# K-nearest-neighbour blocks on one core: neighbour marks turned by DMA instead of TensorE, and the last batch's square row moved to step 0

## What is computed

```python
def _L0_xattn_ref(xyz, points, w_center, w_neighbor):
    ...
    idx = _knn_indices(xyz, K)                 # K = 8 smallest of sq_n + sq_m - 2 x_n.x_m
    idx_t = jnp.transpose(idx, (0, 2, 1))[:, None, :, :]
    for i in range(NUM_BLOCKS):                # 4 blocks
        shortcut = points
        p = _lrelu(points)
        g = _group_point(p, idx_t)             # the 8 neighbours of every point
        c = jnp.einsum('oi,bin->bon', w_center[i], p)
        gn = jnp.einsum('oi,bikn->bokn', w_neighbor[i], g)
        points = (c + gn.sum(axis=2)) / (K + 1.0) + shortcut
    return points
...
    x = _L0_xattn_ref(ctx_4096, x, fside_BxSxS_0, fside_BxSxS_0)
    x = _L1_xattn_ref(ctx_4096, x, fside_BxSxS_0, fside_BxSxS_0)
```

## Time and profile before

| | |
|---|---|
| time, median of 3 runs | 337.64 us (336.52 to 339.07) |
| profiled execution | 334.24 us, of which the span of its instructions is 332.5 us |
| TensorE busy | 320.8 us, 97% of the span |
| VectorE / ScalarE / GpSimd busy | 258.5 / 174.0 / 95.0 us |
| 64 transposes of marks (L385) on TensorE | 4.3 us busy |
| 8 copies `adj<-wide` (L538) on ScalarE | 7.7 us busy |
| DMA | 23.41 MB, nearly all of it in the first 90 us |

### The profile page before, as it was taken

How to read it: one execution, slowest core, us unless ns; L and a number is a source line. 1 busy time by engine, 2 the same in 40 slices (tenths; PEclk the granted TensorE clock), 3 DMA queues, 4 the chain that set the end, 5 groups by cost and what they waited for, 6 DMA issues and landing times.

```text
span 332.5 us, 5114 instructions
## 1 busy us (share of the span) xinstructions
PE 320.8 (97%) x2024; PEld 290.9 (88%) x2024; DVE 258.5 (78%) x333; ACT 174.0 (52%) x255; POOL 95.0 (29%) x85
## 2 busy tenths in 40 slices
PE   4999999999999899999899999999999999999995
PEld 4999999999899788888788889888888888889884
DVE  3994799799699676888867796887869867796773
ACT  4584397485564726454836644626455264644510
POOL 2011111111133214333644441426335063441400
PEclk9999999999999999999999999999999999999999
DMA  7979859969700000000000000000000000000023
GB/s 236 353 209 264 223 146 239 279 150 251 188 0 1 2 0 2 0 0 2 1 2 0 1 3 0 0 2 0 2 0 0 2 0 2 0 0 2 38 92 126
DMA packets 8608, 23.41 MB, mean 70 GB/s; under 512 B 772, under 2 KB 2052, under 8 KB 8584
## 3 DMA queue, kind: packets, MB, share of 16 engines
q1 hardware_dynamic: 7288, 18.36, 16.3%
q0 software_dynamic: 1296, 4.72, 8.3%
HBM read 20.98 MB, written 2.10 MB: 69 GB/s over the span
## 4 chain that ended last, share of the span: by engine, by line
PE 41%; DVE 8%; ACT 2%; issue 1%; DVEq 0%
PE wide L423 24%; PE wide L412 6%; PE wide L401 5%; PE wide L399 5%; DVE y_rest L722 2%; DVE y_lo L726 2%; DVE r_mixed L662 2%; DVE state L734 2%; ACT y_hi L570 2%; ACT relu L562 1%; PE wide L385 0%; ACT r_high L565 0%; DVEq L709 0%; DVEq L725 0%
## 5 line engine op out<-in xcount | busy, mean ns | idle before, releaser
L279 POOL TENSOR_TENSOR r_low<-relu,r_high 128x512 fp32r<-128x512 f32 x64 | 84.8, 1339 | 140.4 <-ACT r_high L565 140.4
L423 PE MATMUL wide<-adj,y_hi 128*128 128x512 f32 (+1 forms) x260 | 102.3, 394 | 0.8 <-DVE state L734 0.8
L423 PE MATMUL wide<-adj,y_lo 128*128 128x512 f32 (+1 forms) x260 | 101.7, 393 | 0.0
L722 DVE TENSOR_TENSOR y_rest<-wide,y_hi 128x1024 f32<-128x1024 f32 x32 | 39.2, 1224 | 45.4 <-ACT y_hi L570 45.4
L562 ACT ACTIVATE relu<-state 128x512 f32<-128x512 f32 x64 | 40.2, 628 | 46.5 <-DVE state L734 33.7
L399 PE MATMUL wide<-w_high,r_high 128*128 128x256 f32 x256 | 62.2, 281 | 0.9 <-DVE y_rest L722 0.9
L401 PE MATMUL wide<-w_low,r_low 128*128 128x256 f32 x256 | 61.9, 280 | 0.0
L570 ACT CAST y_hi<-wide 128x1024 fp32r<-128x1024 f32 x32 | 32.3, 1008 | 54.8 <-PE wide L401 54.8
L423 PEld LDWEIGHTS wide<-adj,y_hi 128*128 128x128 f32 x260 | 48.9, 188 | 11.7 <-DVE state L734 1.2
L423 PEld LDWEIGHTS wide<-adj,y_lo 128*128 128x128 f32 x260 | 49.0, 188 | 10.5 <-issue 0.2
L399 PEld LDWEIGHTS wide<-w_high,r_high 128*128 128x128 f32 x256 | 48.3, 189 | 2.3 <-issue 1.1
(11 more groups left out here) (57 smaller groups left out, 290.6 us busy)
## 6 DMA issues: line engine op xcount, KB each, us to landing
raw<-in_ctx_dram SPq DMA_DIRECT2D x23, 512.0 KB, 5.4
g_low<-in_ctx_dram POOLq DMA_DIRECT2D x9, 512.0 KB, 6.2
state<-in_x_dram SPq DMA_DIRECT2D x4, 512.0 KB, 7.1
out_dram<-state SPq DMA_DIRECT2D x3, 512.0 KB, 2.8
w_raw<-in_fside_BxSxS_dram SPq DMA_DIRECT2D x1, 1024.0 KB, 11.2
rest_raw<-in_ctx_dram SPq DMA_DIRECT2D x4, 130.0 KB
raw<-in_ctx_dram SPq DMA_DIRECT2D x2, 256.0 KB, 3.3
out_dram<-state SPq DMA_DIRECT2D x1, 256.0 KB, 2.0
```

What stands on the lines that cost most here:

```text
L279: nc.gpsimd.tensor_tensor(r_low[:, n % 3, h, :], relu[:, h, :], r_high[:, n % 3, h, :].bitcast(fp32), ALU.subtract).then_inc(r_low_ready, 1)
L423: mm = nc.tensor.matmul(bank[to][:, cols], part[:, s % 2, q, h * P:(h + 1) * P], adj[:, b, q, cols], start=(q == 0 and part is y_hi), stop ...
L722: nc.vector.tensor_tensor(y_rest[:, :, :], wide[MAIN][:, :].rearrange("p (q o) -> p q o", q=NB), y_hi[:, s % 2, :, :].bitcast(fp32), ALU.s ...
```

## The change

The marks are turned by `dma_start_transpose` from `nbr` to a new SBUF tensor `turned`: four DMAs of 128x512 bf16 (128 KB each) per batch, issued by SyncE. ScalarE copies `adj` from `turned`. TensorE's `turn_neighbours` is gone and with it the use of banks 6 and 7 by the marks, so `square_row(b)` waits on `low_copied` in place of `adj_ready`. In SyncE's queue the DMAs for batch 0 stand ahead of the loads of batch 3; those for batches 1, 2 and 3 stand behind all loads. Each set waits for `self_added(b)` and, from batch 1 on, for the copies of the batch before. `copy_adj` comes after `copy_low` in the Gram phase. In the layer phase the work of batch 3 moves one step forward (`square_row` and `distances` to step 0, `turn_distances` and `copy_low` to step 1, `neighbours` to steps 2 to 5, marks to 4 and 6, `add_selves` to 6, `copy_adj(3)` to 8), and `copy_adj(2)` moves one step back, to step 1 behind `copy_low(3)`.

```diff
+        turned = sb("turned", [P, NB, N], bf16)
...
+            def turn_neighbours(b):
+
+                sp.wait_ge(self_added, b + 1)
+                if b > 0:
+                    sp.wait_ge(adj_ready, 2 * b)
+                for i in range(NB):
+                    sp.dma_start_transpose(turned[:, :, i * P:(i + 1) * P], nbr_rows[:, i, :]).then_inc(nbr_turned, 16)
...
             for b in range(1, B):
+                if b == B - 1:
+                    turn_neighbours(0)
                 for k in range(UNITS):
                     load_unit(b, k)
                 load_state(b - 1)
             load_state(B - 1)
+            for b in range(1, B):
+                turn_neighbours(b)
...
             def square_row(b):
 
                 if b > 0:
-                    pe.wait_ge(adj_ready, 2 * b)
+                    pe.wait_ge(low_copied, b * NB)
...
             for b in range(B):
                 main_products(b, 0)
-                if b >= 2:
-                    turn_neighbours(b - 2)
...
                 if s == 0:
-                    turn_neighbours(B - 2)
+                    square_row(B - 1)
                 if s == 1:
-                    square_row(B - 1)
                     pe.wait_ge(gram_ready, B * NB)
...
-                if s == 2:
+                if s == 1:
                     turn_distances(B - 1)
-                if s == ENTER - 1:
-                    turn_neighbours(B - 1)
...
             def copy_adj(b):
+                act.wait_ge(nbr_turned, 16 * NB * (b + 1))
                 for g in range(2):
-                    act.wait_ge(nbr_turned, 2 * b + g + 1)
-                    nc.scalar.copy(adj[:, b, 2 * g:2 * g + 2, :],
-                                   bank[TR_BANKS[g]][:, :].bitcast(bf16).rearrange("p (j n) -> p j n", j=2))\
-                        .then_inc(adj_ready, 1)
+                    nc.scalar.copy(adj[:, b, 2 * g:2 * g + 2, :], turned[:, 2 * g:2 * g + 2, :]).then_inc(adj_ready, 1)
...
                 points_parts(b, 6)
+                copy_low(b - 1)
                 if b >= 2:
                     copy_adj(b - 2)
-                copy_low(b - 1)
...
                 if s == 0:
+                    relu_parts(2)
+                if s == 1:
+                    copy_low(B - 1)
                     copy_adj(B - 2)
-                    relu_parts(2)
-                if s == 2:
-                    copy_low(B - 1)
-                if s == 5:
+                if s == 4:
                     neighbour_marks(B - 1, 0)
-                if s == 7:
+                if s == 6:
                     neighbour_marks(B - 1, 1)
-                if s == ENTER:
+                if s == 8:
                     copy_adj(B - 1)
...
+                if s == 0:
+                    distances(B - 1)
                 if s == 1:
-                    distances(B - 1)
                     relu_mixed(2)
...
-                if 3 <= s < 3 + NB:
-                    neighbours(B - 1, s - 3)
-                if s == 7:
+                if 2 <= s < 2 + NB:
+                    neighbours(B - 1, s - 2)
+                if s == 6:
                     add_selves(B - 1)
```

13 lines of the change are left out of this document (2 added, 11 removed).

## The result

Over four runs each the changed kernel takes 332.5 us (332.0 to 333.85) against 337.6 us (336.52 to 339.07), a ratio of 0.9863 with a 95% interval of 0.9826 to 0.99: 1.4% faster (the quotient of the two medians is 0.985, inside the interval). The profiled executions are closer together than the medians: 332.0 us with a span of 329.9, against 334.24 us with a span of 332.5. So there are two questions: where the 2.6 us between the two profiled spans come from, and why the medians differ by 5.1.

A forecast was written before the change was run, and what follows sets the result against it. TensorE was taken to bound the Gram phase, a ScalarE-VectorE ring steps 3 to 7. Terms -2.7 (Gram phase) + 0.2 (ring start) - 0.9 (ring end) = -3.4 us, from the median 337.64, gave 334.2 us; range 332 to 342.

The forecast's parts named there:

- rival 2: More gained than counted, by quicker ScalarE copies from SBUF and vanishing batch 3 waits: -5, 332.6 us; chance 0.05.
- Transposes out of the Gram phase: Two sets of 16 transposes leave TensorE-bound time, 1.02 us each: 2.0 us gained.
- the square row's wait: TensorE's wait for `copy_adj` before `square_row(2)` in the Gram phase goes: 0.65 us gained.
- VectorE can follow: In the Gram phase VectorE keeps up with the earlier TensorE: cost 0 to +1 us, taken as 0.
- The first rival: VectorE binds at the end of the Gram phase, eating 1 to 2 us: -1.9, 335.7 us; chance 0.10.
- Start of the ring: Steps 0 to 2: relu of step 3 waits for ScalarE's `copy_adj(2)` instead of a state update: +0.2 us.
- The fourth rival: `copy_adj(2)` behind `copy_low(3)` starts the ring 1 us later: -2.4, 335.2 us; chance 0.08.
- The ring: Steps 3 to 8: ScalarE's and VectorE's order sets a 7.15 us period without TensorE; unchanged, 0 us.
- End of the ring: The 16 transposes of batch 3 before `y_step(9)` go: -0.9 us.
- The DMAs: Time T from `add_selves` to landing of a batch's four transposes, taken as 5 to 7 us, costs nothing.
- three marks of a wrong reading: ScalarE idle over 2 us before batch 3's `adj` copy, its first `g_high` awaiting DMA, or transposes over 2 us on SyncE.

The follow-up runs named there:

- the repeated runs: The changed kernel timed again, unaltered, in two later companies beside the kernel before: 332.69 us (ratio 0.989) and 332.87 us (0.9885).
- its order opened: Changed kernel with ScalarE's `y_high(s)` ahead of `relu_parts(s+1)` in steps 3 to 7: 331.62 us, ratio 0.9846 to the kernel before.
- the experiment: Changed kernel with batch 3 alone turned by TensorE again, in step 8, and its `adj` copied in step 9: 333.59 us, ratio 0.991.
- one moved line: Kernel before, with ScalarE's `copy_adj(b-2)` put ahead of `points_parts(b, 5)` and `(b, 6)` in the Gram phase: 334.45 us, ratio 0.9925.
- another kernel: Changed kernel with batch 3's last `g_mixed` earlier on VectorE and `y_high(s)` ahead of `relu_parts(s+1)` in steps 3 to 7: 331.78 us, ratio 0.9859.
- later relu: Changed kernel with ScalarE's relu and `r_high` of step 1 behind `copy_main(3)` and the last marks of batch 2: 333.76 us, ratio 0.9925.
- the transposes twice: Changed kernel with each DMA transpose issued twice, the first into a spare buffer, waiting on both: 341.57 us, ratio 1.0116.
- the old steps: Changed kernel's DMA transposes with the layer phase's order of the kernel before, `copy_adj(2)` in step 0: 334.97 us, ratio 0.9951.

## Why the prediction held, and where its sum did not

The time lies in the range, on the side forecast, but not where the sum put it. 332.5 us is 1.7 under the sum's 334.2 and below its band of 333.2 to 335.2, half a microsecond above the range's lower end, which had been set there for rival 2 (332.6, with a chance of 0.05). That rival's reasons did not come true: the copies from SBUF are not quicker (2.03 us for two, 1.90 from PSUM), and relu of step 3 starts no earlier than the rest has moved. That the range held is in part luck. Against the repeated runs (3.7 and 3.8 us less, for 3.4 in the sum) the sum comes out near, but by two errors that cancel: the wait of the square row is worth more than counted, and VectorE takes 1.0 us back.

- **Transposes out of the Gram phase, 2.0 us, and the square row's wait, 0.65.** In the pair of profiles right: 2.74 measured for 2.7. For the median the wait was the mis-sized term. The step that failed is "since the removed work is the same in each, I take the difference from the median": a wait is not removed work. It was 0.66 us in one execution that was 3.4 us under its median, 3.0 us in a second one, and 2.3 us in the time when it alone was removed. I had read `square_row(1)` as waiting under 0.1 us and counted nothing; in the second execution it waited 1.05 us.
- **VectorE can follow, 0 to +1 us, taken as 0.** The upper end came true: 1.00 us in every profile of the changed kernel. The first rival named the place; its reason, zero slack at the last `g_mixed`, was right, and what made VectorE late is GpSimd's `r_low`, which the sum mentioned and did not price. Its size was also right at the lower end of "1 to 2 us".
- **Start of the ring, +0.2.** Measured 0. The relu of step 3 was released by the `adj` copy, as forecast. The fourth rival did not happen.
- **The ring, 0.** Right: 7.15 us before and after. With its order opened `y_hi` waits for TensorE and the stretch is 1.4 us shorter, so it was the bound, with the next one close behind.
- **End of the ring, -0.9.** 0.98 in the experiment, 0.67 in the pair of profiles, since `r_mixed` of step 8 took 1.80 us there and 1.50 before.
- **The DMAs, T = 5 to 7 us, free.** Batch 3 took 7.1 us, 158.58 to 165.67, and cost nothing measurable. But its parts were wrong in both directions: 1.3 us of issue each, not 0.4, and 4.2 us to landing, not the 1.7 of a store. ScalarE waited 1.06 us before batch 3's copy (0 to 1.6 in the other profiles), under the 2 us set as the mark of a wrong reading, and TensorE did not feel it. The free time there was 6.0 us where 6.7 had been worked out: `add_selves(3)` was taken at 0.42 us, while its row shows 0.91. Batch 1's slack was left out and turned out to be the first to be used up, by a T twice as long and once by a single set that came 3.7 us late.
- **What the profile would show.** Right: no wait of the square row, the period, the releaser of relu 3, and none of the three marks of a wrong reading (one transpose of 16 holds SyncE for 2.95 us, the median is 1.31). Off: `y_step(0)` at 105.27 for 104.3, which is VectorE's 1.0, `y_hi` of step 2 at 122.77 for 122.0, and a landing of 4.2 us for under 3.
- **The rules of the Trainium skill.** "VectorE: DVE Perf Modes" (The three transpose paths) gives 390 ns for a transpose on TensorE; the removed ones were worth 54 ns each, and the trace decides. For its DMA figure of 1309 ns per 128x128 the trace shows a median of 1.31 us of issue for a 128x512, so T was not 21 us; "DMA: Bandwidth & Descriptors" (Latency and other measured facts), with 261 GB/s, made T come near the lower bound, and it did not.

A sum for the median from the parts as they were measured: 2.3 for the wait, 2.0 for the transposes of the Gram phase, 0.6 for the end of the ring, less 1.0 for VectorE: 3.9 us, against 3.7 and 3.8 measured in two companies. The first comparison's 5.1 us lies above this; its before runs spread over 2.55 us, and its interval reaches down to 1.0%.

What stays open: when two instructions of VectorE and GpSimd meet, which of them becomes longer; how often the DMAs of batch 1 land late; and what the moves of the layer phase would do without the DMAs.

## What to carry to other kernels

A wait in one profile is a sample: where the waiting work stands behind another instruction's DMA wait in an engine's queue, its size changes from run to run (0.66 and 3.0 us here), and work that needs no load belongs ahead of work that does. Before an operation is moved to another unit, the order around it is worth a run by itself: here one moved line gives 2.3 of the 3.8 us. When a tuned kernel has two engines tied, a gain on one is read against the slack of the other with the third engine's work beside it, since an overlap that moves makes instructions longer. The transposes moved to a DMA paid because their consumer could be put a full latency later; with the consumers of the layer phase left in place the same kernel gains 1.4 us (336.35 to 334.97), less than the one moved line alone, and with them moved 3.7.

## What the hardware showed

- `DMA_TRANSPOSE` of 128x512 bf16, SBUF to SBUF, holds the issuing SyncE for 1.19 to 2.95 us (median 1.31), where the prediction had taken 0.4 from plain DMAs. Landing takes 2.4 to 7.9 us (11.2 in one profile of another kernel). The 16 of them double the program's packets, from 8608 to 17312, and those under 512 B go from 772 to 9476.
- VectorE and GpSimd together: `g_mixed` 1.21 us alone and 1.83 beside `r_low`, `rest_mixed` 0.69 and 1.68, `half_diag` 0.28 and 1.36, `r_mixed` 1.21 and 2.15. All of these read two tensors in SBUF. `y_rest` and `y_lo`, which read PSUM, keep 1.21 to 1.23 us in all 32 steps, and the searches for neighbours (MAX8, MATCH_REPLACE8), which read one tensor, keep 0.68 to 0.69, beside `r_low` or not. It can also be GpSimd that is held: one `r_low` took 2.87 us in place of 1.29 while `g_mixed` beside it kept its 1.21 (later relu, at 97.94 us).
- A ScalarE copy of 128x1024 bf16 to fp32r takes a little longer from SBUF than from PSUM: 1.08 us against 1.01 in the median of 8, 2.03 against 1.90 for two in a row.
- TensorE's granted clock fell to 0.50 (1.2 GHz) after idle times: from 110 to 115 us behind 4.0 us of idle with the transposes twice, and from 113 to 116 us behind 1.8 us with the old steps, where TensorE was not on the path. With 0.96 us of idle at that place, in the changed kernel, it stayed at 1.00.
